# Moving the look-ahead projection and its transposes within a batch of a three-block decoder layer

## The chip, the cores and the metric

The kernel runs on one core of one Trainium2 chip. The metric is the device time of one execution in microseconds. TensorE (PE in the profile) multiplies matrices, VectorE (DVE), ScalarE (ACT) and GpSimd (POOL) work on elements, and SyncE (SP) issues the DMAs. Each engine works through its own queue in order; semaphores make one engine wait for another.

## The reference

One decoder layer over x of shape (8, 512, 256) with a context of shape (8, 1024, 128). Cut to its steps (weights are fp32):

```python
# block 1: attention without projections per head; q, k, v in bfloat16
xs = depthwise_conv3(x); xs = xs + xs @ pe_w.T
q, k, v = (xs @ qkv_w.T)                # (b, 512, 768), cut in three
# each of them is reshaped (not transposed) to (b, 16 heads, 512, 16)
a = softmax(q @ k.T / sqrt(16)) @ v
x = layernorm(x + a @ out_w.T)
# block 2: causal self attention and cross attention to ctx (1024 tokens), 16 heads of 16
y = causal_attn(x @ Wq + bq, x @ Wk + bk, x @ Wv + bv)
y = y + attn(x @ Wcq + bcq, ctx @ Wck + bck, ctx @ Wcv + bcv)
x = layernorm(x + y @ Wp + bp)
# block 3: routing to one of 64 experts by two arg-max steps over calibrated gates,
# a small spline per token, directions[expert] * magnitude added, two layer norms
x = layernorm(x + ffn(x))
```

Because q, k and v of block 1 are reshaped and not transposed, heads 4i to 4i+3 read the projection of tokens 128i to 128i+127 alone. Such a piece of 128 tokens is called a tile here (tile 0 to 3).

## The kernel before

A batch is one of the 8 sequences. Each engine has a function `batch(b)` that issues its part in a fixed, hand-written order; b runs from 0 to 7. Inside batch b the kernel also does two things for other batches: the routing block of batch b-1 (`prev`), and the first steps of batch b+1 (`ahead`): position projection, q/k projection and v projection.

The order in a batch is this.

1. **First attention**, heads h = 0 to 15. VectorE's `scores1` reads a PSUM bank of scores, scales it to s1 and takes the minimum (L769), ScalarE's `exp1` takes exponentials with their sums (L603), VectorE takes the reciprocal of the sums (`sum1`, L955) and divides three or four tiles of the head (`norm1`, L962), ScalarE divides the fourth for most heads below 14 (L613). DMAs transpose the probabilities of heads 0 to 13 (L411), TensorE those of heads 14 and 15. TensorE's `pv1` (L1330) multiplies with v. In between stand the router work of batch b-1, the context projections for block 2 (`values`, `context_key`) and the position projection of batch b+1. `keep_clock` issues fillers on TensorE whose result nobody reads (L1353).
2. **Between the attentions.** ScalarE's `out1` copies the heads' output out of PSUM (L624), TensorE projects it (L1427), VectorE adds the residual (L1009) and takes the statistics (L774), GpSimd computes the reciprocal deviation, VectorE normalises (L783), TensorE transposes the tokens to features (L1483), ScalarE copies them, and six `unit`s project them to q, k and the cross q (TensorE L1461, ScalarE L643). VectorE does the router's small steps in its gaps: `cluster_choice` (last operation L866), `local_gates`, `expert_choice`.
3. **Score loop** of block 2. TensorE makes the scores twice: once with queries on the partitions for the row maxima (`scores`, L1500 and L1504), once transposed for the probabilities (`scoresT`, L1539 and L1542). VectorE takes the maxima (`maxima(m)`, L1031 and L1034). Slots in PSUM are a ring of four banks, which VectorE frees. The first seven steps of `maxima` (m = 0 to 6) run ahead of the loop proper. ScalarE takes the exponentials (L659), TensorE multiplies bursts of four steps with the values (`pv`, L1557), and VectorE copies each burst out (`outputs(j)`, L1046 and L1049).

The q/k projection of a tile i of batch b+1, `first_qk(b + 1, i)`, has three parts with the same name on three engines:

- TensorE: two fp32 products of 128x128 by 128x512, four passes in the profile (L1228, counted under the helper's line L1205), into the bank `EXTRA_BANKS[QK_AT[i]]`;
- ScalarE: a cast of 128x512 to bf16 in `qk_nat` (L586);
- VectorE: two transposes of 128x512, one for q and one for k (L760). They write q_1 and k_1, which the scores of batch b's first attention read until its last head.

Before the change TensorE issues tile 0 at head 4, tile 1 at head 10 (bank 6, which `pv1` needs from head 13, so TensorE waits for the cast at head 12), tile 2 after the last `pv1`, tile 3 after the v projection. ScalarE's casts follow that. VectorE does all eight transposes in the score loop, a pair each ahead of the copies of bursts 0, 4, 5 and 7:

```python
for j in outputs_ready(s):
    if ahead and j in QK_BURSTS:
        first_qk(b + 1, QK_BURSTS[j])
    outputs(j)
```

Batch 7 has no look-ahead, batch 0 no router work. Before batch 0 the same three functions run once by themselves.

Of the kernel before, what the change touches and what calls it, by code (L numbers as in the profile page):

```python
# [37 lines left out]
def decoder_layer(nc, x, xT, ctxT, conv_w, peT, qkT, vT, outT, Wk, bk, Wq, bq, Wv, bv, Wck, bck, Wcq, bcq,  # L38
# [12 lines left out]
    NT = S // P  # L51
# [29 lines left out]
    BURSTS = STEPS // BURST  # L81
    CHUNKS = 16
    EXTRAS = KD + NT + 2
    EXTRA_BANKS = (7, 4, 7, 6, 0, 5, 7, 1)
    QK_ORDER, V_AT = (0, 1, 2, 3), 5
    QK_AT, QK_TURN = (2, 3, 4, 7), [QK_ORDER.index(i) for i in range(NT)]
    QK_BURSTS = {0: 0, 4: 1, 5: 2, 7: 3}
    OUT_BANK, WEIGHT_PARTS = 2, 3
    A1_BANKS, E1_SLOTS = 4, 5
    FILLERS = 8  # L90
# [4 lines left out]
    PV1_BANKS = (4, 6)  # L95
# [20 lines left out]
    with ctx:  # L116
# [49 lines left out]
        o1T = sb("o1T", [P, KD, S], bf16)  # L166
# [389 lines left out]
        def _(act):  # L556
# [25 lines left out]
            def first_qk(b, i):  # L582

                e = QK_AT[i]
                act.wait_ge(ex_mm, b * EXTRAS + e + 1)
                nc.scalar.copy(qk_nat[:, i, :, :, 0:HD], bank[:, EXTRA_BANKS[e], :].rearrange("p (a c j) -> p a c j", a=2, j=HD)).then_inc(qk_cast, 1)  # L586

# [6 lines left out]
            def batch(b, prev=True, ahead=True):  # L594
# [26 lines left out]
                def out1(k):  # L621

                    act.wait_ge(o1_mm, b * H + 8 * (k + 1))
                    nc.scalar.copy(o1T[:, k, :].rearrange("p (r c) -> p r c", c=CHUNKS),  # L624
                                   bank[:, PV1_BANKS[k], :].rearrange("p (c r) -> p r c", c=CHUNKS)).then_inc(o1_copied, 1)

                def features():
                    for k in range(KD):
# [33 lines left out]
                for h in range(H):  # L662
                    exp1(h)
                    if h >= 1:
                        norm1(h - 1)
                    if h == 12:
                        out1(0)
                    if prev:
                        if h == 1:
                            y_features(0, featA, c)  # L670
                    if ahead and h == 4:
                        first_qk(b + 1, 0)
                    if prev:
                        if h == 4:
                            y_features(1, featB, c)
                        if h == 6:
                            gate_exps(c)
                        if h == 7:
                            hidden(c)
                    if 0 <= h - 8 < 2 * CTX_UNITS:  # L680
                        context_key(h - 8)
                    if ahead and h == 10:
                        first_qk(b + 1, 1)
                for h in range(BY_DMA, H):
                    transposed_half(h)
                out1(1)
# [7 lines left out]
                features()  # L694
                unit(0, 0)
                unit(1, 0)
                unit(0, 1)
                unit(1, 1)
                units(2)
# [16 lines left out]

            act.wait_ge(pad_ready, 3)
            first_qk(0, 0)
            first_qk(0, 1)
            first_qk(0, 2)  # L720
            first_v(0)
            first_qk(0, 3)
            act.wait_ge(w_in, W_IN)
            act.wait_ge(const_ready, 1)
            act.wait_ge(sig_ready, SIG_STEPS)
# [9 lines left out]
        def _(dve):  # L735
# [205 lines left out]
            def batch(b, prev=True, ahead=2):  # L941
# [61 lines left out]
                if prev:  # L1003
                    cluster_pick(sf)
                    cluster_choice(c, sf)
                dve.wait_ge(xn_in, b * 16 + 16)
                for i in range(2):
                    dve.wait_ge(out_mm, b * 2 + i + 1)
# [8 lines left out]
                if prev:  # L1017
                    local_gates(c, sf, 1)
                    expert_choice(c, sf)

                def maxima(m):

# [49 lines left out]
                for m in range(LEAD):  # L1072
                    if m == NT + 2:
                        put_rows(SELF, 0)
                    maxima(m)
                    if prev and m == EXPERT_LEAD:
                        expert_columns(base, uses)
                    if m in VALUES_LEAD:
                        values(CTX_PAIRS + VALUES_LEAD.index(m))
                    if prev and m == GATHER_LEAD:  # L1080
                        compressed(c)
                    if prev and m == SPLINE_LEAD:
                        spline(c, sf)
                for s in range(ALL_STEPS):
# [10 lines left out]
                    for m in range(maxima_before(s), maxima_before(s + 1)):  # L1095
                        maxima(m)
                    for j in outputs_ready(s):
                        if ahead and j in QK_BURSTS:
                            first_qk(b + 1, QK_BURSTS[j])
                        outputs(j)  # L1100
                    for part in rows_behind(s):
                        put_rows(*part)
# [95 lines left out]
        def _(pe):  # L1198
# [110 lines left out]
            def batch(b, prev=True, ahead=True):  # L1309
# [81 lines left out]
                for h in range(2, H):  # L1391
# [22 lines left out]
                        values((h - 8) // 2)  # L1414
                    if h in (9, 11, 13, 15):
                        context_key((h - 9) // 2)
                    if h == 9 or h in (10, 11) and not ahead:
                        keep_clock(6, FILLERS // 2)
                    if ahead and h == 10:
                        first_qk(b + 1, 1)  # L1420
                    if ahead and h == 12:
                        pe.wait_ge(qk_cast, (b + 1) * NT + 2)

                def tokens(t, k):

# [60 lines left out]
                pe.wait_ge(o1_copied, (b + 1) * KD)  # L1486
                unit(0)
                unit(1)

                def scores(m, r):  # L1490

# [77 lines left out]
                    last.then_inc(slot_in, 1)  # L1569

                if ahead:
                    pe.wait_ge(qk_cast, (b + 2) * NT)
                for m in range(LEAD):
                    if m == NT + 2:
                        max_rows(SELF, 0)
# [59 lines left out]
            for m in range(KD):  # L1635
                position(0, m)
            first_qk(0, 0)
            first_qk(0, 1)
            first_qk(0, 2)
            first_v(0)  # L1640
            first_qk(0, 3)
            pe.wait_ge(const_ready, 1)
            pe.wait_ge(w_in, W_IN)
            pe.wait_ge(sig_ready, 5)
# [51 lines left out]
```

## Time and profile before

| what | value |
|---|---|
| time, median of 3 runs | 2367.22 us (2365.92 to 2370.24) |
| the profiled execution | 2367.22 us, its span 2365.5 us |
| TensorE busy | 2178.3 us, 92% of the span |
| VectorE busy | 1874.9 us, 79% |
| ScalarE busy | 1382.4 us, 58% |
| GpSimd busy | 189.6 us, 8% |
| mean granted TensorE clock | 0.948 of full speed |

The profile is one execution. Busy time is the time in which an engine had an instruction at work; the idle time ahead of an instruction is put down to what released it. TensorE's passes are pipelined: the time from one start to the next tells what a pass costs the queue, its own duration is longer. The granted clock is 1.00 (2.4 GHz) or 0.50 (1.2 GHz) at any moment.

### The profile page before, as it was taken

The page shows a single profiled execution, that of the slowest core. Times are in us where ns is not written, and L with a number is a line of the kernel's source. Part 1 is how long each engine was busy: PE and PEld are TensorE (multiplying, and loading weights), DVE is VectorE, ACT ScalarE, POOL GpSimd, SP SyncE. Part 2 cuts the span into 40 slices and gives each one's busy share as a digit, 9 for nine tenths or more (in the row PEclk, how much of TensorE's full clock was granted, in tenths as well). Part 3 has the DMA queues.
Part 4 walks back from the last instruction along what each step waited for, and adds up shares of the span by engine and source line. Part 5 has one row for each costly group of instructions (what it writes and reads, how often), then busy time and mean ns, then how long its engine had stood idle before and what let it go on. Part 6 is the DMA issues. An engine that isn't in the chain of part 4 may idle for free.

```text
span 2365.5 us, 37053 instructions
## 1 busy us (share of the span) xinstructions
PE 2178.3 (92%) x12810; PEld 1003.4 (42%) x12810; DVE 1874.9 (79%) x5149; ACT 1382.4 (58%) x2977; POOL 189.6 (8%) x349
## 2 busy tenths in 40 slices
PE   4899988999889998999989998899988999889992
PEld 1254434543345433454335443454334543345432
DVE  5858869788878879788797887978878886878854
ACT  2844677456754578446784467735676457744650
POOL 3011001100011000110001100100001100001000
PEclk7899999999999999999999999989999999789995
DMA  3600024000430006100160002400042000510000
GB/s 108 125 10 1 1 55 89 10 1 1 101 51 10 1 19 116 25 4 1 37 116 10 1 1 66 87 10 1 1 88 55 10 1 10 98 36 1 1 10 9
DMA packets 250843, 81.65 MB, mean 35 GB/s; under 512 B 236064, under 2 KB 247328, under 8 KB 250656
## 3 DMA queue, kind: packets, MB, share of 16 engines
q1 hardware_dynamic: 250656, 79.29, 16.3%
q8 instruction: 102, 1.67, 0.3%
q14 instruction: 85, 0.70, 0.1%
HBM read 16.35 MB, written 4.19 MB: 9 GB/s over the span
## 4 chain that ended last, share of the span: by engine, by line
PE 77%; DVE 11%; ACT 8%; issue 3%; DMA 1%; SPq 0%; POOL 0%; DVEq 0%; POOLq 0%; ACTq 0%
PE bank L1504 22%; PE bank L1557 13%; PE bank L1542 8%; PE bank L1205 8%; PE bank L1500 5%; PE bank L1461 4%; DVE work L769 4%; PE bank L1539 4%; ACT work L603 4%; PE bank L1330 2%; PE bank L1317 2%; PE bank L1517 2%; PE bank L1568 1%; ACT work L659 1%; PE bank L1296 1%
## 5 line engine op out<-in xcount | busy, mean ns | idle before, releaser
L659 ACT ACTIVATE work<-bank 128x512 f32<-128x512 f32 (+3 forms) x1536 | 737.5, 552 | 557.8 <-PE bank L1542 288.2
L1034 DVE TENSOR_REDUCE top_half<-bank 128x1 f32<-128x512 f32 x1024 | 625.0, 679 | 18.5 <-PE bank L1504 18.5
L1504 PE MATMUL bank<-k_c,q_c 32*128 32x512 f32 x2048 | 626.9, 631 | 0.0
L1542 PE MATMUL bank<-q_c,k_c 32*128 32x512 f32 x2048 | 548.9, 629 | 0.0
L603 ACT ACTIVATE work<-work,neg 128x512 bf16<-128x512 bf16 x512 | 363.3, 720 | 60.8 <-DVE work L769 60.8
L1504 PEld LDWEIGHTS bank<-k_c,q_c 32*128 32x128 f32 x2048 | 274.4, 183 | 245.4 <-DVE top_half L1034 159.5
L769 DVE TENSOR_SCALAR_CACHE_REDUCE work<-bank 128x512 bf16<-128x512 f32 x512 | 322.0, 685 | 71.1 <-PE bank L1317 38.7
L1557 PE MATMUL bank<-work,v_flat 128*32 128x512 f32 (+3 forms) x3072 | 316.9, 547 | 9.2 <-ACT work L659 8.8
L1031 DVE CUSTOM_DVE_ANT_0 masked<-bank,mask_w 128x384 bf16<-128x384 f32 (+3 forms) x512 | 223.3, 488 | 68.0 <-PE bank L1500 64.0
L1542 PEld LDWEIGHTS bank<-q_c,k_c 32*128 32x128 f32 x2048 | 227.0, 183 | 92.5 <-ACT work L659 57.2
L1539 PE MATMUL bank<-q_s,k_s 32*128 32x512 f32 (+3 forms) x1024 | 257.2, 470 | 0.0
L1500 PE MATMUL bank<-k_s,q_s 32*128 32x128 f32 (+3 forms) x1024 | 198.5, 481 | 8.4 <-ACT k_s L643 7.6
L1557 PEld LDWEIGHTS bank<-work,v_flat 128*32 128x32 f32 x3072 | 91.1, 110 | 235.6 <-issue 131.7
L1317 PE MATMUL bank<-k,q 32*128 32x512 bf16 x448 | 136.4, 396 | 29.3 <-DVE work L769 17.7
L1330 PE MATMUL bank<-work,v 128*32 128x512 bf16 x512 | 137.9, 396 | 17.8 <-DMA work<-work 17.8
L1539 PEld LDWEIGHTS bank<-q_s,k_s 32*128 32x128 f32 x1024 | 142.0, 184 | 20.1 <-ACT work L659 9.1
L1500 PEld LDWEIGHTS bank<-k_s,q_s 32*128 32x128 f32 x1024 | 104.1, 188 | 88.2 <-issue 41.4
L518 POOL TENSOR_SCALAR ln_var<-mv 128x4 f32<-128x4 f32 x32 | 8.7, 273 | 1539.8 <-DVE mv L778 1539.8
L529 POOL TENSOR_SCALAR_AFFINE_SELECT work<-work 128x512 f32<-128x512 f32 x128 | 81.6, 637 | 601.7 <-ACT work L659 601.7
L962 DVE TENSOR_SCALAR work<-work,rden 128x512 bf16<-128x512 bf16 x424 | 123.0, 349 | 4.5
L1046 DVE COPY featA<-bank 128x512 f32<-128x512 f32 x64 | 44.3, 692 | 90.9 <-PE bank L1557 90.9
L603 ACT ACTIVATION_READ_ACCUMULATOR work<-work,neg 128x1 bf16 x512 | 103.5, 202 | 0.0
(191 smaller groups left out, 2205.7 us busy)
## 6 DMA issues: line engine op xcount, KB each, us to landing
xT_pad<-xT SPq DMA_DIRECT2D x16, 256.0 KB, 3.3
ctx_sb<-ctxT SPq DMA_DIRECT2D x8, 512.0 KB, 3.3
x_res<-x SPq DMA_DIRECT2D x8, 512.0 KB, 4.8
out<-r_sb SPq DMA_DIRECT2D x8, 512.0 KB, 3.1
work<-work SPq DMA_TRANSPOSE x112, 4.3
qk_sb<-qkT SPq DMA_DIRECT2D x1, 512.0 KB, 4.8
pe_sb<-peT SPq DMA_DIRECT2D x1, 256.0 KB, 4.1
v_sb<-vT SPq DMA_DIRECT2D x1, 256.0 KB, 5.2
```

What stands on the lines that cost most here:

```text
L603: nc.scalar.activation(e1[:, h % E1_SLOTS, t, :], s1[:, h % 2, t, :], ACT.Exp, bias=neg1[:, h % 2, t:t + 1], scale=-1.0, accum_out=den1[:, ...
L659: nc.scalar.activation(pT[:, s % PT_SLOTS, g, q0:S], exp_bank(n)[:, 0:S - q0], ACT.Exp, scale=SCALE).then_inc(pT_ready, 1)
L769: nc.vector.tensor_scalar(s1[:, h % 2, t, :], bank[:, (NT * h + t) % A1_BANKS, :], -SCALE, None, ALU.mult, ALU.min, accum_out=neg1[:, h % ...
L1031: nc.vector.tensor_tensor_reduce(masked[:, g, 0:n], scores[:, 0:n], mask_w[:, S - n:S], -1.0, -MASKED, ALU.add, ALU.min, top_s[:, i % 2, u ...
L1034: nc.vector.tensor_reduce(top_half[:, i % 2, g, u // 2, u % 2:u % 2 + 1], scores, AX.X, ALU.max, negate=True).then_inc(slot_out, 1)
L1205: last = mm(dst, lhsT(k), rhs(k), start=(k == 0), stop=(k == tiles - 1))
L1330: last = mm(bank[GW * g:GW * (g + 1), PV1_BANKS[h // 8], :], v1[:, h, j, :], p1T[:, h % E1_SLOTS, :, j, :], start=(h % 2 == 0 and j == 0), ...
L1500: mm(dst[:, 0:n], q_s[rows, i, P * u:n], k_s[rows, i, 0:n], start=True, stop=True, tile_position=(GW * g, 0)).then_inc(slot_in, 1)
L1504: mm(dst, q_c[rows, i, P * t:P * (t + 1)], k_c[rows, i, S * half:S * (half + 1)], start=True, stop=True, tile_position=(GW * g, 0)).then_i ...
L1539: mm(dst[:, 0:S - q0], k_s[rows, i, q0:q0 + P], q_s[rows, i, q0:S], start=True, stop=True, tile_position=(GW * g, 0)).then_inc(sT_mm, 1)
L1542: mm(dst, k_c[rows, i, P * u:P * (u + 1)], q_c[rows, i, :], start=True, stop=True, tile_position=(GW * g, 0)).then_inc(sT_mm, 1)
L1557: last = mm(dst[GW * g:GW * (g + 1), q0:S], v_flat[:, at:at + GW], pT[:, s % PT_SLOTS, g, q0:S], start=(s % BURST == 0), stop=(s % BURST = ...
```

## The change

- Tile 1 of the q/k projection leaves head 10 of the first attention. TensorE issues it after unit 1, ScalarE casts it after the first halves of units 0 and 1. The order of the tiles becomes 0, 2, 3, 1, and the banks are renumbered so that each tile keeps its bank. Before the first scores of block 2 TensorE waits for three casts, not four.
- In its place the fillers of heads 9 to 12 become 4, 2, 4, 2 in every batch. Before they were 4 at head 9, and 4 each at heads 10 and 11 in the last batch alone.
- VectorE's four pairs of transposes leave the score loop. They stand before the residual add (tile 0), before `maxima(0)` (tile 2), after `maxima(0)` (tile 3) and after `maxima(1)` (tile 1).
- `out1` walks both sides in the other order: it reads PSUM in a row and writes o1T with a stride of 16 elements, where it read with a stride of 32 elements and wrote in a row. The elements and their places are the same.

```diff
-    EXTRA_BANKS = (7, 4, 7, 6, 0, 5, 7, 1)
-    QK_ORDER, V_AT = (0, 1, 2, 3), 5
-    QK_AT, QK_TURN = (2, 3, 4, 7), [QK_ORDER.index(i) for i in range(NT)]
-    QK_BURSTS = {0: 0, 4: 1, 5: 2, 7: 3}
+    EXTRA_BANKS = (7, 4, 7, 0, 5, 7, 1, 6)
+    QK_ORDER, V_AT = (0, 2, 3, 1), 4
+    QK_AT, QK_TURN = (2, 7, 3, 6), [QK_ORDER.index(i) for i in range(NT)]
...
# ScalarE, out1
-                    nc.scalar.copy(o1T[:, k, :].rearrange("p (r c) -> p r c", c=CHUNKS),
-                                   bank[:, PV1_BANKS[k], :].rearrange("p (c r) -> p r c", c=CHUNKS)).then_inc(o1_copied, 1)
+                    nc.scalar.copy(o1T[:, k, :].rearrange("p (r c) -> p c r", c=CHUNKS),
+                                   bank[:, PV1_BANKS[k], :].rearrange("p (c r) -> p c r", c=CHUNKS)).then_inc(o1_copied, 1)
...
# ScalarE, batch
-                    if ahead and h == 10:
-                        first_qk(b + 1, 1)
...
                 unit(0, 0)
                 unit(1, 0)
+                if ahead:
+                    first_qk(b + 1, 1)
                 unit(0, 1)
...
# ScalarE and TensorE, before batch 0
             first_qk(0, 0)
-            first_qk(0, 1)
             first_qk(0, 2)
             first_v(0)
             first_qk(0, 3)
+            first_qk(0, 1)
...
# VectorE, batch
                     cluster_choice(c, sf)
+                if ahead:
+                    first_qk(b + 1, 0)
                 dve.wait_ge(xn_in, b * 16 + 16)
...
                     expert_choice(c, sf)
+                if ahead:
+                    first_qk(b + 1, 2)
...
                     maxima(m)
                     if prev and m == EXPERT_LEAD:
                         expert_columns(base, uses)
+                    if ahead and m in (0, 1):
+                        first_qk(b + 1, QK_ORDER[2 + m])
...
                     for j in outputs_ready(s):
-                        if ahead and j in QK_BURSTS:
-                            first_qk(b + 1, QK_BURSTS[j])
                         outputs(j)
...
# TensorE, batch
-                    if h == 9 or h in (10, 11) and not ahead:
-                        keep_clock(6, FILLERS // 2)
-                    if ahead and h == 10:
-                        first_qk(b + 1, 1)
-                    if ahead and h == 12:
-                        pe.wait_ge(qk_cast, (b + 1) * NT + 2)
+                    if 9 <= h < 13:
+                        keep_clock(6, 4 if h % 2 else 2)
...
                 unit(0)
                 unit(1)
+                if ahead:
+                    first_qk(b + 1, 1)
...
                 if ahead:
-                    pe.wait_ge(qk_cast, (b + 2) * NT)
+                    pe.wait_ge(qk_cast, (b + 1) * NT + 3)
```

## Rows read from the trace of the kernel before

**Rows 1.** The page: the chain that ended last, its shares by engine.
```profile
PE 77%; DVE 11%; ACT 8%; issue 3%; DMA 1%; SPq 0%; POOL 0%; DVEq 0%; POOLq 0%; ACTq 0%
```

**Rows 2.** Windows, us: length, busy time per engine, granted clock, DMA share, GB/s.
```profile
399.70:680.50 280.80, 267.70 (x1602) 123.78 (x1601) 233.33 (x640) 172.65 (x372) 22.27 (x40) 0.97 0.17 35
680.50:962.80 282.30, 268.68 (x1603) 124.48 (x1601) 233.43 (x640) 172.52 (x372) 22.26 (x40) 0.97 0.17 35
962.80:1242.80 280.00, 266.29 (x1603) 123.23 (x1601) 233.53 (x640) 172.53 (x372) 22.26 (x40) 0.98 0.17 35
...
1522.80:1807.00 284.20, 271.03 (x1602) 125.40 (x1601) 233.62 (x641) 172.71 (x372) 22.26 (x40) 0.96 0.16 32
...
987.20:994.00 6.80, 6.80 (x16) 3.21 (x18) 3.67 (x15) 0.27 (x1) 0.00 (x0) 0.50 0.00 0
703.90:714.10 10.20, 10.20 (x29) 6.19 (x30) 5.15 (x20) 1.17 (x2) 0.00 (x0) 0.50 0.00 0
```

**Rows 3.** Timeline of VectorE in batch 3's score loop: start, duration, [idle before].
```profile
1016.46 0.71 DVE L760 STREAM_TRANSPOSE q<-qk_nat 128x512 bf16<-128x512 bf16 x1
1017.09 0.67 DVE L760 STREAM_TRANSPOSE k<-qk_nat 128x512 bf16<-128x512 bf16 x1
...
1018.98 0.69 DVE L1046 COPY featA<-bank 128x512 f32<-128x512 f32 x1 [1.22 <-PE bank L1557]
...
1077.92 0.69 DVE L1046 COPY featA<-bank 128x512 f32<-128x512 f32 x1 [1.00 <-PE bank L1557]
```

**Rows 4.** Timeline of TensorE in batch 3's first attention, heads 9 to 11.
```profile
925.66 1.03 PE L1353 MATMUL bank<-k,identb 128*128 128x512 bf16 x4
...
929.51 1.88 PE L1205 MATMUL bank<-qk_sb,xs 128*128 128x512 f32 x4
931.33 1.03 PE L1317 MATMUL bank<-k,q 32*128 32x512 bf16 x4
```

**Rows 5.** Waits from 923.9 to 956.3 us: in total, times, longest.
```profile
DVE rden L955 <- ACT work L603: 0.5, 2, 0.2
```

**Rows 6.** Timeline of VectorE around batch 3's residual add.
```profile
961.72 0.61 DVE L866 TENSOR_REDUCE gates<-work 128x32 f32<-128x256 f32 x1
...
962.82 0.69 DVE L1009 TENSOR_TENSOR x_res<-x_res,bank 128x512 f32<-128x512 f32 x1 [0.49 <-PE bank L1427]
...
963.74 0.69 DVE L1009 TENSOR_TENSOR x_res<-x_res,bank 128x512 f32<-128x512 f32 x1 [0.22 <-PE bank L1427]
```

**Rows 7.** Timeline of batch 3 from unit 1 to the third maxima.
```profile
972.70 1.88 PE L1461 MATMUL bank<-featB,wk_sb 128*128 128x512 f32 x4
...
975.53 0.50 PE L1500 MATMUL bank<-k_s,q_s 32*128 32x128 f32 x8 [0.96 <-ACT k_s L643]
...
976.18 0.29 DVE L1031 CUSTOM_DVE_ANT_0 masked<-bank,mask_w 128x128 bf16<-128x128 f32 x1 [1.08 <-PE bank L1500]
...
978.77 0.42 DVE L1031 CUSTOM_DVE_ANT_0 masked<-bank,mask_w 128x256 bf16<-128x256 f32 x1 [1.59 <-PE bank L1500]
...
981.71 0.69 DVE L969 TENSOR_TENSOR v_flat<-bank,bv_row 128x512 f32<-128x512 f32 x1 [0.88 <-PE bank L1205]
...
982.70 0.56 DVE L1031 CUSTOM_DVE_ANT_0 masked<-bank,mask_w 128x384 bf16<-128x384 f32 x1 [0.30 <-PE bank L1500]
```

**Rows 8.** Groups of instructions by form, ScalarE: busy us, mean ns, idle before.
```profile
L659 ACT ACTIVATE work<-bank 128x512 f32<-128x512 f32 x1152 | 606.1, 606 | 346.7 <-PE bank L1542 288.2 <-PE bank L1539 54.6 <-PE bank L1504 2.2
...
L659 ACT ACTIVATE work<-bank 128x128 f32<-128x128 f32 x128 | 35.5, 278 | 132.0 <-PE bank L1539 132.0
...
L586 ACT CAST qk_nat<-bank 128x512 bf16<-128x512 f32 x32 | 18.5, 581 | 19.4 <-PE bank L1205 19.4
...
L624 ACT CAST o1T<-bank 128x512 bf16<-128x512 f32 x16 | 9.4, 585 | 11.8 <-PE bank L1330 11.8
```

**Rows 9.** Timeline before batch 0: TensorE's q/k passes, ScalarE's first casts.
```profile
20.39 5.42 PE L1205 MATMUL bank<-qk_sb,xs 128*128 128x512 f32 x12 [1.38 <-DVE xs L753]
...
23.75 1.07 ACT L586 CAST qk_nat<-bank 128x512 bf16<-128x512 f32 x2
```

More of the change, by code:

```diff
@@ L1637, in _ @@
             first_qk(0, 0)
-            first_qk(0, 1)
             first_qk(0, 2)
@@ L1641, in _ @@
             first_qk(0, 3)
+            first_qk(0, 1)
             pe.wait_ge(const_ready, 1)
```

## The prediction

> **What bounds the kernel now.** I read the page first. The chain of work that ended last is TensorE's for 77% of the span [rows 1], so what counts is what TensorE waits for and what stands in its queue. Then I took windows from one residual add to the next: the batches repeat, with 280.8, 282.3, 280.0, 280.0 and 284.2 us from batch 1 on (the fourth, from batch 4, equals the third and has no row) [rows 2]. So the steps below are read in the timeline of batch 3 (961 to 1243 us). The idles that I use stand at the same places of batches 1 to 6 within 0.02 us.
>
> Three stretches matter. In the first attention, heads 8 to 13 keep VectorE and ScalarE without a pause, and TensorE waits for them. Between the two attentions short steps are handed from engine to engine. In the score loop TensorE streams, and VectorE waits for it at every PV burst.
>
> **Four pairs of transposes leave the score loop: 0.** A pair takes 1.30 us of VectorE (1016.46 to 1017.76), and four pairs a batch stand ahead of the copy of a burst. After the pair VectorE still idles 1.22 us until TensorE's burst ends; over the four places the idle is 1.00 to 1.22 [rows 3]. The pair lies in time that is waited anyway: removing 28 pairs (4 in each of 7 batches, 36 us) gives nothing. That burst is the cover; were it gone, each pair would be worth its 1.30. Bounds: 0 and a gain of 36 us.
>
> **Tile 1 leaves the first attention: -0.45 a batch.** Its four passes occupy TensorE for 1.82 us (929.51 to the next start, 931.33). Eight more fillers replace them (a row of four spans 1.03 with its drain, so eight take about 1.9), and TensorE has waits for VectorE around them [rows 4]: no change there. On ScalarE the cast of 0.58 goes. VectorE waits for ScalarE only twice here, at heads 11 and 13, 0.5 us in all (0.23 and 0.22 in the timeline) [rows 5]. With ScalarE 0.58 ahead both waits go, and then VectorE has no gap left and bounds the stretch. Bounds 0 and -0.58. The last batch has 12 fillers before and after: 0.
>
> **The pair for tile 0 stands before the residual add: +0.50.** VectorE ends the cluster choice at 961.72 + 0.61 = 962.33 and waits for TensorE until 962.82; the second add starts at 963.74, after 0.22 of waiting [rows 6]. With the pair, the first starts at 963.63 and the second, one add of 0.61 later, at 964.24. Behind it in VectorE's queue stand the statistics and the normalisation, for which GpSimd's rstd and then TensorE's token transposes wait in turn, so the 0.50 goes on. The pair's data was cast 50 us before. Bounds: 0 and 1.30. In batch 0, without router work, VectorE waits 5 us there: 0.
>
> **Tile 1 stands between unit 1 and the first scores: +0.80.** Unit 1 starts at 972.70, and four such passes free the queue after 1.81 us, at 974.51. Scores(0) start at 975.53, having waited 0.96 for ScalarE's k_s [rows 7]. Tile 1's 1.82 us fill that wait and more: scores(0) start at 976.33. Unit 2, scores(1) and all else of the batch stand behind them, and from here on TensorE seldom waits, so the 0.80 isn't won back. Its cast on ScalarE comes ahead of units (0,1) and (1,1), which are first read at step 4. Bounds: 0.8 and 1.82.
>
> **The other three pairs: 0.** That for tile 2 stands where VectorE waits 1.08 for scores(0), which now come 0.80 later: 1.88 us hold 1.30. That for tile 3 stands where it waits 1.59 for scores(1). That for tile 1 stands ahead of the value add, which waits 0.88: the add comes 0.42 late, the maxima behind it had a wait of 0.30 of their own, and 0.12 is left over, which I leave out [rows 7]. Bounds: 0 and 0.4 a batch.
>
> **out1's layout: 0.** The copy read PSUM with a stride and wrote a row; now it reads a row and writes every 16th element. The strided read took 585 ns, the contiguous one of the same size in the q/k cast 581 [rows 8], so nothing is gained on the read. No row shows the strided write. If the part that grows with the elements doubled, that would be (606 - 278) / 384 x 512 = 0.44 us [rows 8] for each of 16 copies, 7.0 us if all were bare. The second copy of a batch is covered by tile 2's 1.82 us on TensorE, the first partly by ScalarE's new lead. I take 0, near the cast, which also writes in pieces; the bounds are 0 and 7.0.
> The Trainium skill (SBUF — State Buffer, Door 1: The DMA port swizzle) says that accesses which cross to a new 16-byte line pay a penalty, and that PSUM has lines of 8 bytes; that would make the new write the slower one. For the read, the trace does not show such a penalty on ScalarE (585 against 581 ns).
>
> **The start: +0.4.** TensorE ran 12 passes in 5.25 us and then found tile 0's cast done. With 8 passes it gets there at 23.9, and the cast that starts at 23.75 is done at 24.3 [rows 9]. The rest of the work is the same, and VectorE's setup behind the last transpose is bare. Bounds 0 and 0.6.
>
> **The sum.** Batches 1 to 6: -0.45 + 0.50 + 0.80 = +0.85 each, 5.1 in all. Batch 0: +0.35. Start +0.4. Together +5.85. The profiled execution took 2367.22 us (span 2365.5 and 1.7 around it), which is also the median of the runs: so 2373.1 us, +0.25%. 0.2%, about what a measurement of this kernel can tell from no change, is 4.7 us: the borders are 2362.5 and 2371.9.
>
> **The clock.** In each batch the granted clock falls from 1.00 to 0.50 some 24 us after the residual add, after small matmuls and waits: 6.8 us long in batch 3, 10.2 in batch 2 (and 6). Batch 2 also has a dip before it, batch 5 one in its loop [rows 2]. Against 280.0, the extras cost 0.8 + 2.3 + 4.2 = 7.3 us in batches 1 to 6. How a batch lies against the moments of switching decides on them, and the change moves that. I expect as many as before; the bounds are -7.3, and +3.1 (batch 2's two) in four more batches, +12.
>
> **The rivals.**
> A, no change (0.33): ScalarE's whole 0.58 comes through and the pair costs 0.2 rather than 0.50, net +0.42 a batch, 2370 us; or the extras at half clock vanish, 2373.1 - 7.3 = 2365.8.
> B, faster (0.12): tile 1's dense 1.82 us in the wait between the attentions keep the clock at 2.4 GHz behind them. A stretch of 6.8 us at 1.2 GHz costs 3.4 us; without it in 6 batches the time is 2373.1 - 20.4 = 2352.7. It passes the border of 2362.5 from four batches on. Against it: the 1.82 us end 11 us before the fall, and the waits in between stay. For it: batches 2 and 5 show how little moves a dip.
> The Trainium skill (TensorE: Matmul & The Clock Gate, Part 1) says that the default state is throttled and that activity releases it; the falls in this trace do follow waits.
> B2, faster (0.05): VectorE bounds the loop after all, and part of the 36 us is won. It decides where the idle before the copies is 0; it is 1.0 to 1.2.
> C, much slower (0.12): the strided write costs its 7.0 us, or the half clock is 10.2 us long in four more batches (2.3 each, 9.2): 2380 to 2382.
> The forecast: 0.38.
>
> **The numbers.** The range takes in A and C, and below it the extras gone with A: 2362 to 2382. Slower by over 0.2%: C and most of the forecast, 0.45. Within: A and the forecast's lower end, 0.35. Faster: B, B2 and a lucky clock with A, 0.20.
>
> **What would show it.** VectorE's idle ahead of the PV copies grows from 1.2 to 2.5 us; its waits for ScalarE in heads 10 to 13 are gone; the second residual add starts 2.52 us after the start of the choice's last reduction, not 2.02; scores(0) start 3.63 us after unit 1, not 2.83, with no wait for k_s; out1's copy stays near 585 ns; a batch without extras takes 280.85 us. I am wrong if it takes 280.0 or less, or if the half clock has another length in most batches.

## The result, and the profile after

The changed kernel takes 2397.15 us in the median of 4 runs (2385.14 to 2401.06), against 2367.98 us for the kernel before, timed beside it: a ratio of 1.0116 (95% interval 1.0084 to 1.0149), slower by 20 to 35 us. Forecast were 2373.1 us and a range of 2362 to 2382. The direction was right; the size lies outside the range, above the worst rival (C, 2380 to 2382). The profiled execution took 2390.6 us, with a span of 2388.9.

The page's row of the chain that ended last, by engine, is the first sign: TensorE has two points less than before and ScalarE three more [rows 1].

```profile
PE 75%; ACT 11%; DVE 9%; issue 3%; DMA 1%; SPq 0%; POOL 0%; DVEq 0%; POOLq 0%; ACTq 0%
```

One row decides. It is that of ScalarE's `out1` copy (L623 now): the copy's least, middle and longest duration in ns, and below it who waited for it.

```profile
L623 ACT CAST o1T<-bank x16: 2309/2336/2368, 106.4 to 2111.8; 128x512 bf16<-128x512 f32 x16
its engine sat idle before it (us, times) until:
  PE bank L1333: 11.8, 8
who waited for it (us, times):
  PEld bank L1426: 12.2, 8
  PE bank L1426: 6.0, 8
```

It took 585 ns before [rows 8] and 2336 now, 1.75 us more in each of 16 copies. TensorE's output projection waits for it in all eight batches; in the kernel before, there is one such wait, 0.7 us long.

The timeline of batch 3 of the changed kernel (start, duration, [idle before]) shows where both copies go. The first copy:

```profile
952.31 2.35 ACT L623 CAST o1T<-bank 128x512 bf16<-128x512 f32 x1
...
957.94 0.18 DVE L954 RECIPROCAL rden<-den 128x4 f32<-128x4 bf16 x1 [1.56 <-ACT work L602]
```

It stands in ScalarE's queue ahead of the exponentials of a late head, and VectorE now waits 1.56 us for them, where both its waits for ScalarE in heads 8 to 13 had been 0.5 together [rows 5]. The second copy, to the residual add:

```profile
970.72 2.33 ACT L623 CAST o1T<-bank 128x512 bf16<-128x512 f32 x1 [1.47 <-PE bank L1333]
...
972.59 0.61 DVE L865 TENSOR_REDUCE gates<-work 128x32 f32<-128x256 f32 x1
...
973.10 2.14 PE L1426 MATMUL bank<-out_b,o1T 128*128 128x256 bf16 x18 [0.51 <-ACT o1T L623]
973.12 0.70 DVE L759 STREAM_TRANSPOSE q<-qk_nat 128x512 bf16<-128x512 bf16 x1
...
973.74 0.67 DVE L759 STREAM_TRANSPOSE k<-qk_nat 128x512 bf16<-128x512 bf16 x1
974.36 0.69 DVE L1010 TENSOR_TENSOR x_res<-x_res,bank 128x512 f32<-128x512 f32 x1
...
975.27 0.69 DVE L1010 TENSOR_TENSOR x_res<-x_res,bank 128x512 f32<-128x512 f32 x1 [0.22 <-PE bank L1426]
```

Tile 2's pass, which I counted as the cover, ends, and TensorE then waits 0.51 for the copy; even with a pair of transposes ahead of it the second add still waits for TensorE. The second add starts 2.68 us after the last reduction of the choice; it was 2.02 [rows 6], and I had written 2.52.

From unit 1 to the first scores, in the same timeline:

```profile
984.23 1.88 PE L1460 MATMUL bank<-featB,wk_sb 128*128 128x512 f32 x4
...
985.95 1.88 PE L1208 MATMUL bank<-qk_sb,xs 128*128 128x512 f32 x4
...
987.76 0.50 PE L1501 MATMUL bank<-k_s,q_s 32*128 32x128 f32 x8
...
988.43 0.29 DVE L1034 CUSTOM_DVE_ANT_0 masked<-bank,mask_w 128x128 bf16<-128x128 f32 x1 [0.58 <-PE bank L1501]
...
990.99 0.42 DVE L1034 CUSTOM_DVE_ANT_0 masked<-bank,mask_w 128x256 bf16<-128x256 f32 x1 [0.35 <-PE bank L1501]
```

Scores(0) start 3.53 us after unit 1 and wait for nothing; before it was 2.83 with 0.96 of waiting [rows 7]. That is +0.70 for a forecast of +0.80. The waits of the maxima, 1.08 and 1.59 before [rows 7], are now 0.58 and 0.35: the pairs lie in them.

In the score loop, the copy of the first burst (the first row is of the timeline, the second the page's group over the whole execution: busy, mean ns, idle before):

```profile
1029.58 0.69 DVE L1049 COPY featA<-bank 128x512 f32<-128x512 f32 x1 [2.44 <-PE bank L1558]
```

```profile
L1049 DVE COPY featA<-bank 128x512 f32<-128x512 f32 x64 | 44.3, 692 | 105.4 <-PE bank L1558 105.4
```

The kernel before has 90.9 us of idle there:

```profile
L1046 DVE COPY featA<-bank 128x512 f32<-128x512 f32 x64 | 44.3, 692 | 90.9 <-PE bank L1557 90.9
```

Where the pair was, VectorE idles 2.44 us instead of 1.22 [rows 3]. The pairs turned into waiting, as forecast.

The windows from one residual add to the next, batches 1 to 5:

```profile
407.70:691.00 283.30, 270.51 (x1609) 124.24 (x1609) 233.30 (x641) 175.60 (x372) 22.21 (x40) 0.96 0.17 34
691.00:974.40 283.40, 270.66 (x1609) 124.33 (x1609) 233.45 (x642) 175.59 (x372) 22.20 (x40) 0.96 0.17 34
974.40:1257.80 283.40, 270.65 (x1608) 124.22 (x1609) 233.34 (x642) 175.60 (x372) 22.20 (x40) 0.96 0.17 34
1257.80:1544.60 286.80, 274.05 (x1608) 125.15 (x1609) 233.58 (x641) 175.67 (x372) 22.21 (x40) 0.95 0.16 34
1544.60:1828.00 283.40, 271.15 (x1609) 123.46 (x1609) 233.47 (x642) 175.56 (x372) 22.20 (x40) 0.96 0.16 32
```

Batch by batch, that is +2.5, +1.1, +3.4, +6.8 and -0.8 against before [rows 2]. ScalarE's busy time in batch 3 grew by 3.1 us (172.5 to 175.6), most of what two copies at +1.75 give.

How much of this lies on the path can be read between the same instructions of both timelines. Batch 3 from the reciprocal of a late head (L955, L954 now) to the statistics behind the residual add, before and then in the changed kernel:

```profile
923.27 0.17 DVE L955 RECIPROCAL rden<-den 128x4 f32<-128x4 bf16 x1
...
964.46 1.41 DVE L774 BATCH_NORM_STATS2 stats<-x_res 128x6 f32<-128x256 f32 x4
```

```profile
933.13 0.18 DVE L954 RECIPROCAL rden<-den 128x4 f32<-128x4 bf16 x1
...
976.00 1.41 DVE L773 BATCH_NORM_STATS2 stats<-x_res 128x6 f32<-128x256 f32 x4
```

From the first row to the choice's last reduction it is 38.45 us before and 39.46 now (+1.0), from there to the statistics 2.74 and 3.41 (+0.7), and from the statistics to the first maxima 11.72 and 12.43 (+0.7). Together that is 2.4 us, for 3.4 by which the batch from this add to the next is longer. That batch has 20.5 us of half clock and had 13.7.

### The profile page after: what moved, and what is told of

Its sections match the earlier page's. It is cut to its first block, busy times and chain, and to the rows that moved or that the text cites. A ratio compares the mean times of both kernels' runs of the same rounds, so it can differ in the third digit from the quotient of the medians.

```text
span 2388.9 us, 37143 instructions
## 1 busy us (share of the span) xinstructions
PE 2205.1 (92%) x12850; PEld 1006.5 (42%) x12866; DVE 1876.4 (79%) x5149; ACT 1406.9 (59%) x2977; POOL 189.1 (8%) x349
## 4 chain that ended last, share of the span: by engine, by line
PE 75%; ACT 11%; DVE 9%; issue 3%; DMA 1%; SPq 0%; POOL 0%; DVEq 0%; POOLq 0%; ACTq 0%
PE bank L1505 22%; PE bank L1558 13%; PE bank L1543 8%; PE bank L1208 7%; ACT work L602 6%; PE bank L1501 5%; PE bank L1460 4%; PE bank L1540 4%; DVE work L768 3%; PE bank L1333 2%; PE bank L1518 2%; ACT o1T L623 2%; PE bank L1320 1%; PE bank L1569 1%; ACT work L658 1%
## 5 line engine op out<-in xcount | busy, mean ns | idle before, releaser
L1333 PE MATMUL bank<-work,v 128*32 128x512 bf16 x512 | 145.2, 413 | 6.1 <-DMA work<-work 5.7
```

The source lines that it names most:

```text
L1333: last = mm(bank[GW * g:GW * (g + 1), PV1_BANKS[h // 8], :], v1[:, h, j, :], p1T[:, h % E1_SLOTS, :, j, :], start=(h % 2 == 0 and j == 0), ...
```

## The experiments

Each is timed against the kernel before on its chip. A ratio's interval is of 95%; us are the ratio's distance from 1 times 2370. Half-clock sums and batch lengths are those of the profiled executions.

### Which part of the change costs it

`e1_old_out1` is the changed kernel with the old copy:

```diff
-                    nc.scalar.copy(o1T[:, k, :].rearrange("p (r c) -> p c r", c=CHUNKS),
-                                   bank[:, PV1_BANKS[k], :].rearrange("p (c r) -> p c r", c=CHUNKS)).then_inc(o1_copied, 1)
+                    nc.scalar.copy(o1T[:, k, :].rearrange("p (r c) -> p r c", c=CHUNKS),
+                                   bank[:, PV1_BANKS[k], :].rearrange("p (c r) -> p r c", c=CHUNKS)).then_inc(o1_copied, 1)
```

> The changed kernel with out1's copy back as it was: a strided read of PSUM and a row written. Theory W (the strided write is the cause: the copy took 2.34 us in the changed kernel against 0.585 before): the copy takes 0.585 us again, and of the 29 us that were lost only the forecast's own terms stay, so 2373 us (ratio 1.0025, 0.999 to 1.005). Theory M (the moved work is the cause: tile 1 on TensorE ahead of the first scores and the pair ahead of the residual add, with the half clock that follows from them): most of the loss stays, 2388 us or more (ratio 1.008 or more).

Measured: 1.003 (1.0018 to 1.0043), +7.1 us; the forecast without the write was +5.9. The copy is back at 585 ns. So theory W holds and theory M is out: some 20 of the change's 27 us go with the copy's write.

`e2_new_out1_only` is the kernel before with those two lines of the change alone, the reverse of that diff.

> The kernel before with out1's new copy and nothing else. Theory W: the copy takes 2.34 us; the second copy of a batch has 1.1 us of cover, so 0.6 to 0.7 us are bare, and the first lies on ScalarE, which VectorE waits for in the heads behind it, so 1.5 us: 2.2 us a batch, 17 to 20 us in all, 2386 us (ratio 1.007 to 1.009). Theory M: the copies are hidden, ratio within 1.002.

Measured: 1.0114 (1.0098 to 1.0129), +27 us, as much as the whole change and above the 17 to 20 that theory W gave. The copy's row and batch 3's timeline:

```profile
L624 ACT CAST o1T<-bank x16: 2305/2336/2375, 102.8 to 2116.4; 128x512 bf16<-128x512 f32 x16
```

```profile
950.18 2.35 ACT L624 CAST o1T<-bank 128x512 bf16<-128x512 f32 x1
...
955.80 0.18 DVE L955 RECIPROCAL rden<-den 128x4 f32<-128x4 bf16 x1 [1.72 <-ACT work L603]
...
968.58 2.33 ACT L624 CAST o1T<-bank 128x512 bf16<-128x512 f32 x1 [1.47 <-PE bank L1330]
...
970.97 2.14 PE L1427 MATMUL bank<-out_b,o1T 128*128 128x256 bf16 x18 [0.51 <-ACT o1T L624]
...
973.14 0.69 DVE L1009 TENSOR_TENSOR x_res<-x_res,bank 128x512 f32<-128x512 f32 x1 [0.22 <-PE bank L1427]
```

From the first copy to the second it is 18.4 us, from there to the second add 4.56. In batch 3 before, it was 16.9 (copies at 942.96 and 959.86) and 3.88. So the first copy puts 1.5 us on the path and the second 0.7, 2.2 of the 3.5 that both grew by; in the last batch the second puts 1.5 on it. That is 18 us over eight batches, short of the 27 by 9 and of the interval's lower end (23) by 5. The half clock sums to 291 us, against 247 in the kernel before.

### The write's price against its stride

`e5_stride_sweep` takes the kernel before, reads PSUM in a row throughout, and gives the write another stride in each batch. The elements then land in the wrong places and the rest of the layer is computed from them; the sizes of the copies stay. It was timed once, so only its rows are used.

```diff
-                    nc.scalar.copy(o1T[:, k, :].rearrange("p (r c) -> p r c", c=CHUNKS),
-                                   bank[:, PV1_BANKS[k], :].rearrange("p (c r) -> p r c", c=CHUNKS)).then_inc(o1_copied, 1)
+                    run = (1, 2, 4, 8, 16, 32, 64, 128)[b]
+                    nc.scalar.copy(o1T[:, k, :].rearrange("p (r c) -> p c r", c=run),
+                                   bank[:, PV1_BANKS[k], :].rearrange("p (c r) -> p c r", c=run)).then_inc(o1_copied, 1)
```

> The kernel before, with out1's copy walking PSUM in a row and writing o1T with a stride of 1, 2, 4, 8, 16, 32, 64 and 128 bf16 elements in batches 0 to 7, so the rest of the layer is computed from values in the wrong places; 16 copies of 128x512. Theory L (accesses that cross to a new 16-byte line are what costs): 0.585 us up to a stride of 4 elements (8 bytes), a part of the extra at 8, the full 2.34 us from 16 elements on. Theory S (every write that is not next to the last costs, whatever the stride): 2.34 us from a stride of 2 on. Theory B (only large strides, by the bank of the memory): a cost that goes on rising beyond 16.

Measured, one row for each of batches 0 to 5 (strides 1, 2, 4, 8, 16 and 32 elements); 64 and 128 gave 2452 and 2426 ns:

```profile
L625 ACT CAST o1T<-bank x2: 573/579/585, 108.0 to 124.9; 128x512 bf16<-128x512 f32 x2
...
L625 ACT CAST o1T<-bank x2: 732/732/733, 382.6 to 399.6; 128x512 bf16<-128x512 f32 x2
...
L625 ACT CAST o1T<-bank x2: 1302/1309/1316, 666.1 to 684.5; 128x512 bf16<-128x512 f32 x2
...
L625 ACT CAST o1T<-bank x2: 2443/2445/2447, 949.3 to 967.8; 128x512 bf16<-128x512 f32 x2
...
L625 ACT CAST o1T<-bank x2: 2326/2352/2379, 1232.8 to 1251.2; 128x512 bf16<-128x512 f32 x2
...
L625 ACT CAST o1T<-bank x2: 2403/2413/2423, 1519.4 to 1537.9; 128x512 bf16<-128x512 f32 x2
```

The time nearly doubles from stride 2 to 4 and from 4 to 8, and is flat within 5% from 8 elements on, which are 16 bytes. Theory L has the end of the rise right and its start wrong (it had 585 ns up to stride 4); S and B are out. At strides 2, 4 and 8 the write comes to another 16 bytes 128, 256 and 512 times, and each further time costs 4.4 to 4.5 ns (577 / 128 and 1136 / 256): an estimate from these rows, which prices such a write. The cast of the q/k projection writes in pieces of 16 elements in a row and pays nothing (581 ns, [rows 8]). So it is not "a strided write" that costs, but how few elements each 16 bytes take.
The Trainium skill (SBUF — State Buffer, Door 1: The DMA port swizzle) gives SBUF lines of 16 bytes and a penalty for each access that crosses to a new one. The rows agree on the line: nothing gets worse beyond 16 bytes. It also says that two hits in a line reach full bandwidth; there the measurement decides otherwise, since stride 4 has two elements in 16 bytes and takes 1309 ns against 579.

### The moves, one without the other

`e3_tile1_moved_only` moves tile 1, banks and fillers, and leaves the pairs in the loop:

```diff
+    QK_BURSTS = {0: 0, 4: 2, 5: 3, 7: 1}
...
-                    if ahead and h == 10:
-                        first_qk(b + 1, 1)
...
+                    if 9 <= h < 13:
+                        keep_clock(6, 4 if h % 2 else 2)
...
                 unit(1)
+                if ahead:
+                    first_qk(b + 1, 1)
```

> The kernel before with tile 1 moved on TensorE and ScalarE and the fillers of the change; out1 and the transposes of VectorE (in the score loop, in the order 0, 2, 3, 1) as before. Forecast: -0.45 in the first attention, +0.80 ahead of the first scores (0.70 was read in the trace of the changed kernel): +0.35 in each of 7 batches and +0.4 at the start, so 2371 us (ratio 1.001). Rival, the clock: tile 1's dense passes keep the clock up behind them, ratio under 0.997. Theory M: 1.005 or more.

`e4_pairs_moved_only` takes the pairs out of the loop and leaves tile 1 where it was:

```diff
+                if ahead:
+                    first_qk(b + 1, 0)
                 dve.wait_ge(xn_in, b * 16 + 16)
...
+                if ahead:
+                    first_qk(b + 1, 1)
...
+                    if ahead and m in (0, 1):
+                        first_qk(b + 1, 2 + m)
...
-                        if ahead and j in QK_BURSTS:
-                            first_qk(b + 1, QK_BURSTS[j])
```

> The kernel before with VectorE's four pairs of transposes at the four new places and nothing else. Forecast: +0.50 for the pair ahead of the residual add, and, since the first scores do not come 0.80 later here, 1.30 - 1.08 = 0.2 for the second pair: +0.7 in each of batches 1 to 6, 4 us, 2372 us (ratio 1.0018). Rival: the score loop was bound by VectorE and gains up to 36 us, ratio under 0.998.

Measured: e3 1.0026 (1.0014 to 1.0037), +6.2 us; e4 1.0046 (1.0032 to 1.0061), +10.9. My steps give +2.9 for the first kernel (0.35 in seven batches and 0.4 at the start) and +3.0 for the second (4 in its expectation, with 0.2 for the second pair). Both cost more than that, and together (e1, +7.1, at most 10.2) they cost less than their sum of 17 (at least 11).

On the path they do add up. Batch 3 of e1:

```profile
930.82 0.17 DVE L954 RECIPROCAL rden<-den 128x4 f32<-128x4 bf16 x1
...
968.76 0.61 DVE L865 TENSOR_REDUCE gates<-work 128x32 f32<-128x256 f32 x1
...
971.79 1.40 DVE L773 BATCH_NORM_STATS2 stats<-x_res 128x6 f32<-128x256 f32 x4
...
984.22 0.29 DVE L1034 CUSTOM_DVE_ANT_0 masked<-bank,mask_w 128x128 bf16<-128x128 f32 x1 [0.59 <-PE bank L1501]
```

Against the kernel before, the first stretch is 0.5 us shorter (37.94 for 38.45), the second 0.3 longer (3.03 for 2.74), the third 0.7 longer (12.43 for 11.72): +0.5 a batch, where the forecast had +0.85. The same stretches give +0.2 in e3 (first and third) and +0.3 in e4 (second). Over the batches that is about 1.5, 2 and 3.5 us for e3, e4 and e1. The rest, some 5, 9 and 4 us, comes with 24, 21 and 31 us more of half clock, and it is this part that doesn't add up.

### Is it the clock

Batch 3 before has a stretch of 6.8 us at half clock 24 us after the residual add [rows 2]. It begins in the router's gather (64x65 and 64x256 products), 4 us behind the eight products of two columns each that make the compressed features. `e7_fillers_at_gather` puts four fillers behind those eight, ahead of the gather (bank 7, free at that step); `e11_two_fillers_at_gather` two, `e12_eight_fillers_at_gather` eight; `e6_fillers_before_pv12` puts five elsewhere, behind the first `out1` copy and before head 12's product; `e8_both_fillers` has e6's and e7's.

```diff
# e7; e11 has 2, e12 has 8
                         compressed(c)
+                        keep_clock(7, 4)
...
# e6
+                pe.wait_ge(o1_copied, b * KD + 1)
+                keep_clock(4, 5)
```

> The kernel before, with five fillers on TensorE where it waits 1.76 us for the DMA of head 12 (they write a bank that nobody reads then). If half clock follows such waits, the dip 11 us ahead of the residual add is gone in every batch, worth up to 3 us in a batch that has it, 2 to 3 batches a run: ratio 0.996 to 0.999. If it hangs on something else: 1.000, since the fillers stand in a wait.

> The kernel before, with four fillers (0.9 us) behind the compressed features' matmuls, ahead of the half clock of 6.8 us that each batch has there. If they lift it: 3.4 us back less 0.4 to 0.9 in each of 7 batches, 17 us or more, ratio 0.993. If not: 0.4 to 0.9 us lost in 7 batches, ratio 1.001 to 1.003.

> Both sets of fillers. If the two dips are separate, the sum of the two changes; if the dips hang together through the position of a batch against the moments of switching, more than the sum. It also is the base for a later run with the strided copy, in which the clock would have less part.

> The kernel before with two fillers at the gather in place of four. If the half clock falls by the work of TensorE ahead of it and two are enough, 0.992 again or 0.2 us a batch better; if not, between 0.993 and 1.001, with the half clock still there in some batches.

> The same with eight fillers. Four more cost 0.86 us in each of 7 batches if they stand bare, 6 us: 0.995. If four leave some half clock that eight lift, up to 0.990.

| kernel | ratio | interval | us |
|---|---|---|---|
| e6, 5 before head 12 | 1.0016 | 1.0006 to 1.0025 | +3.8 |
| e7, 4 at the gather | 0.9924 | 0.9906 to 0.9943 | -18.0 |
| e8, both | 0.9936 | 0.9922 to 0.9951 | -15.2 |
| e11, 2 at the gather | 0.9901 | 0.9886 to 0.9916 | -23.5 |
| e12, 8 at the gather | 0.9929 | 0.9914 to 0.9944 | -16.8 |

Windows of batch 3 around the gather. The kernel before, and then e11, each from 20.0 us after its residual add; the 0.77 or 1.00 is the granted clock:

```profile
982.80:997.80 15.00, 15.00 (x58) 8.00 (x58) 9.96 (x43) 3.10 (x5) 0.00 (x0) 0.77 0.00 1
```

```profile
981.50:996.50 15.00, 14.56 (x70) 8.18 (x70) 11.15 (x47) 3.99 (x7) 0.00 (x0) 1.00 0.00 1
```

TensorE has 70 recorded matmuls in the same 15 us instead of 58, and only two fillers were put in. The unit behind the gather shows it, before and then in e11:

```profile
989.91 3.78 PE L1461 MATMUL bank<-featB,wk_sb 128*128 128x512 f32 x4
```

```profile
987.30 1.98 PE L1461 MATMUL bank<-featB,wk_sb 128*128 128x512 f32 x4
```

The same four passes take 3.78 us at 1.2 GHz and 1.98 at 2.4. Summed over the profiled execution, half clock lasts 247 us before and 190 in e11, and its span is 18 us shorter (2347.4 against 2365.5). Only fillers were added, so the gain is the clock's: about a third of a us of span for each us of half clock that goes. Two fillers are as good as four or better. Eight lie above two (-16.8 against -23.5), with intervals that just overlap. Fillers in both places (e8) give about the sum of e6 and e7.

Before head 12 they only cost. In the kernel before, batches 1 and 5 have 3.4 us of half clock each, some 10 us ahead of the next residual add. In e6 no batch has that. Yet its half clock sums to 254 us, against 247, since other stretches came, and its time is above both forms of its expectation. So a stretch that is taken away at one place can return at another, and only the sum and the time tell.
The Trainium skill (TensorE: Matmul & The Clock Gate, Part 1) calls the throttled state the default, which activity releases; the full clock behind two fillers that feed nothing agrees with that.

`e18_two_fillers_again` repeats e11 on another chip.

> The kernel before with two fillers at the gather, once more, as the base of the next two on the same chip: 0.990 (0.989 to 0.992).

Measured: 0.9878 (0.9851 to 0.9904), -29 us; 2347.97 us. The gain holds, and two fillers in the kernel before are the fastest version found, ahead of both kernels.

### The write and the moves, with the dips filled

`e9_new_out1_and_gather_fillers` is e2 with four fillers, `e10_moves_and_gather_fillers` e1 with four; `e16_moves_two_fillers` is e1 and `e17_change_two_fillers` the whole change with two.

```diff
                         compressed(c)
+                        keep_clock(7, 4)   # 2 in e16 and e17
```

> The kernel before with out1's strided copy and the four fillers at the gather; to be set against the fillers alone (0.992, 2355 us). The strided copy has put off the end of the heads by 1.50 us and the residual add by 0.69 in the trace, 2.2 us a batch, 17.5 us in all, while it cost 27 us in time with about 43 us more at half clock. If the half clock at the gather had the rest of the loss, the difference here is 17 to 20 us: 2373 us, ratio 1.000. If the loss is the copy's alone, it is 27 us again: 2381 us, ratio 1.004.

> The changed kernel with out1's old copy and the four fillers at the gather; to be set against the fillers alone (0.992, 2355 us). Forecast of the moves without the clock: +5.9 us, so 2361 us, ratio 0.995. If the moves' price was mostly half clock at the gather, they cost under 3 us here: 0.993. If the fillers have taken waits that the moves counted on, over 10 us: 0.997.

> The changed kernel with out1's old copy and two fillers at the gather. If the moves themselves cost 0.85 us a batch as forecast: 5.9 us over the base, 0.9925. If their price in the kernel before was half clock alone: 0.990 as the base, and a candidate for the fastest version.

> The changed kernel as it is, with the strided copy, and two fillers at the gather. Against the run above it shows what the strided copy costs with the clock kept up: 2.2 us a batch, 17.5 us, would give 0.997 to 1.000; with four fillers it was 11 us, 0.995.

| kernel | ratio | interval | us |
|---|---|---|---|
| e9, write + 4 | 0.9971 | 0.9958 to 0.9985 | -6.9 |
| e10, moves + 4 | 0.9916 | 0.9895 to 0.9937 | -19.9 |
| e16, moves + 2 | 0.9908 | 0.9884 to 0.9932 | -21.9 |
| e17, change + 2 | 1.0004 | 0.9990 to 1.0018 | +1.0 |

The write's cost is the difference of two kernels: 27 us alone (e2), 20 with the moves (the change less e1), 11 with four fillers (e9 less e7, under the 17 to 27 of its expectation), 23 with two fillers and the moves (e17 less e16), each good to some 5 us, the second to 8. Its 18 us on the path lie among them, and the clock adds to them or takes from them. The moves cost 7 us without fillers and nothing that shows with four (e10 against e7). With two, e16 lies 2 us above e11 and 7 above e18, and the intervals overlap: open.

### A known delay

If a delay moves the dips, one that does nothing else must cost more or less than itself. `e13_delay_1`, `e14_delay_2` and `e15_delay_4` add VectorE operations of 0.61 us each, whose result nobody reads, between the residual add and the statistics of every batch.

```diff
+                for i in range(4):   # 1 in e13, 2 in e14
+                    nc.vector.tensor_tensor(masked[:, i, :], mask_w[:], mask_w[:], ALU.add)
```

> The kernel before, with one addition of 0.61 us on VectorE between the residual adds and the statistics of every batch, where all engines wait for it. If a bare delay is simply added: 8 x 0.61 = 4.9 us, 2377 us where the kernel before has 2372, ratio 1.002. If a batch takes up a small delay in a jump of some 3.3 us (periods between residual adds of 280.0, 283.3 and 286.8 us have been the common ones, whatever was changed): the periods are 283.3 in nearly all batches, where the kernel before has 280.0 in three or four, ratio 1.004 to 1.006.

> The same with two additions, 1.22 us a batch. Simply added: 9.8 us, ratio 1.0041, periods of 281.2. Jumps: periods of 283.3 again, hardly longer than with one addition, ratio 1.004 to 1.006.

> The same with four additions, 2.44 us a batch, near the 2.2 us that the strided copy has cost in the trace. Simply added: 19.5 us, ratio 1.0082, periods of 282.4. Jumps: periods of 283.3 and 286.8, as with the strided copy, ratio 1.009 to 1.012.

Timeline of VectorE in batch 3 of e15:

```profile
978.22 0.69 DVE L1009 TENSOR_TENSOR x_res<-x_res,bank 128x512 f32<-128x512 f32 x1 [0.23 <-PE bank L1429]
978.94 2.50 DVE L1014 TENSOR_TENSOR masked<-mask_w 128x512 bf16<-128x512 f32 x4
981.36 1.40 DVE L774 BATCH_NORM_STATS2 stats<-x_res 128x6 f32<-128x256 f32 x4
```

| delay a batch | in eight batches | ratio | us measured |
|---|---|---|---|
| 0.61 us | 4.9 | 1.0037 (1.0024 to 1.0050) | 5.7 to 11.9 |
| 1.22 us | 9.8 | 1.0053 (1.0037 to 1.0069) | 8.8 to 16.4 |
| 2.44 us | 19.5 | 1.0158 (1.0140 to 1.0176) | 33 to 42 |

The first costs more than its own length by at least 0.8 us; the second's interval holds its own; the last costs about twice. Its half clock sums to 306 us against 247. So a delay of 2.4 us a batch is answered by 18 us on top, and in one kernel with everything else as before.

The expectations also had a form in which batches grow by jumps. With one addition batches 1 to 5 take 284.3, 282.4, 284.6, 282.0 and 284.0 us, not 283.3 in nearly all; with two, 284.1, 282.6, 283.2, 283.3 and 284.3, near it; with four, 286.1 to 291.5, above it. Neither form fits all three.

## Why the prediction was wrong

**The step that failed** is "out1's layout: 0", and with it the end of its bound, 0.44 us a copy and 7.0 in all. The copy grew by 1.75 us, four times the bound. The term was mis-sized, not misplaced: I made an upper bound from a row whose per-element cost I doubled, and nothing in the trace showed that doubling was the most. The q/k cast "which also writes in pieces" was the wrong neighbour: its pieces are 32 bytes in a row, out1's are 2. What stands beside the sum from the Trainium skill (SBUF — State Buffer, Door 1: The DMA port swizzle), that a crossing to a new 16-byte line pays, pointed the right way; it has no price there, and I let the unshown price be small. With 1.75 us, the same steps would have given +5.9 and about 18: 2391 us, inside the measured interval (2388 to 2403 on a kernel before of 2367.98). That would have been luck in part, since the moves' terms were too large and the clock's too small, as below.

The range had a fault of its own. The bounds that the prediction gives, 7.0 for the copies and 12 for the clock, reach 2392 together; rival C took one or the other, and the range ended at 2382.

**The cover was overestimated too.** The second copy "is covered by tile 2's 1.82 us on TensorE": all but 0.5 us of it on TensorE; yet after it the output projection and two adds follow bare, and 0.7 us come through. As for "the first partly by ScalarE's new lead": the lead can win its half us only once, and the sum had spent it on tile 1 (-0.45). In e2, without the lead, the first copy adds 1.6 us to the heads; in the changed kernel the heads grow by 1.0.

**Rival C** named the right mechanism with a chance of 0.12 and that same too small price. Rivals A, B and B2 did not occur. B's claim that dense work between the attentions removes the dip was wrong as placed. e3 tests it by itself: it has tile 1 there and takes 1.0026, where this rival wanted under 0.997, and its batch 3 still has the 6.8 us of half clock at the gather. The idea was right some 9 us later in the batch: fillers ahead of the gather remove that dip and 15 to 29 us of time.

**Steps that held.** Four pairs out of the loop, 0: the idle ahead of the copy grew by nearly their length (1.22 to 2.44). Tile 1 out of the first attention, -0.45: -0.5. Tile 1 before the scores, +0.80: +0.7, under its lower bound. The other pairs, 0: the maxima's waits hold them.

**A step that was too large.** The pair ahead of the residual add, +0.50: +0.3 in e1. In e4 it is +0.3 too. Pair and adds follow each other there without a wait, each starting a little before the last has ended. In the changed kernel it adds nothing of its own, since the copy is later still. So a batch's moves are +0.5 and not +0.85, about 3.5 us in all and not 5.85; that e1 measures +7.1 (4 to 10), near the forecast, is the clock's doing. The start's +0.4 can't be read: the first residual add comes at 122.5 us in e13 and 126.8 in e11, with the same work ahead of it.

**The clock: "as many as before"** did not hold. No batch takes 280.85 us; half clock grew by 41 us, in e3 and e4 by 24 and 21, and their costs don't add up. In the profiled execution of the changed kernel most is path: 2.4 us in each of eight batches, 19 of the span's growth of 23.4 (an estimate from batch 3). That leaves 4 for 41 us more of half clock, far less than the third of a us each that e11 gained: where the half clock lies counts, and not only how long it is. In e2 (27 for 18) and e15 (37 for 19.5) the clock has a clear part.

**What stays open**: how much of the change's 27 us (20 to 35) is path and how much clock: the path read in batch 3 gives 19, and one profiled execution stands for it. The four pairs of kernels put the write between 11 and 27 around its 18, with intervals that don't allow a finer split. Why a given delay adds dips in one kernel and loses them in another was not settled.

## What to carry to other kernels

When a change reverses the two sides of a copy, look at which side has its elements in a row within 16 bytes, and time the copy by itself before anything else; a bound made by doubling the nearest row is not a bound. Where the clock drops at the same place of every batch, look for the row of small matmuls ahead of it: two fillers behind them took off 1.0 to 1.2%, while five at another place cost 0.2%. And when half-clock stretches sit on the path, expect a delay to cost up to twice its length, as the longest one here did, so compare variants by timed runs rather than by summed microseconds.

## What the runs showed of the hardware

- ScalarE writing bf16 to SBUF, 128x512 from PSUM: 579, 732, 1309 and 2445 ns at strides of 1, 2, 4 and 8 elements, and 2352 to 2452 at 16 to 128. Reading fp32 from PSUM at stride 32 takes 585 ns, 579 in a row.
- Two fillers (half of e7's four, which take 0.97 us of TensorE) between the eight two-column products and the gather kept the granted clock at 1.00 over the 15 us in which it had been 0.77, and took 1.0 to 1.2% off the time.
- A VectorE delay of 2.44 us a batch, 19.5 in all, cost 33 to 42 us.
